# A causal mask moved into unused contraction rows: four 64x64 products on a diagonal block

## The reference, cut to what matters

```python
scores = jnp.einsum('bhqd,bhkd->bhqk', q, k) / math.sqrt(hd)
causal = jnp.tril(jnp.ones((l, l), bool))
scores = jnp.where(causal, scores, -jnp.inf)
att = jax.nn.softmax(scores, axis=-1)
out = jnp.einsum('bhqk,bhkd->bhqd', att, v)
```

## Time and profile before

| | us |
|---|---|
| three runs | 2000.06, 2002.21, 2006.18 (median 2002.21) |
| span of the profiled execution | 2000.6 |
| its time outside the span | not in the profile; the median run is 1.6 longer than the span |
| busy in the span: TensorE, VectorE, ScalarE, POOL | 1867.0, 1487.5, 1038.1, 635.2 |
| attention with its output projection | about 165 to 640 |

### The profile page before, as it was taken

The page is one execution under the profiler, slowest core; times in us unless marked ns, Lnnn a source line. Parts: engine busy times, 40 slices in busy tenths (PEclk is TensorE's granted clock), DMA queues, the critical chain, the costliest instruction groups (busy, mean ns, idle before and its releaser), DMA issues. The chain is left out here.

```text
span 2000.6 us, 40100 instructions
## 1 busy us (share of the span) xinstructions
PE 1867.0 (93%) x15312; PEld 1158.9 (58%) x15312; DVE 1487.5 (74%) x2424; ACT 1038.1 (52%) x1973; POOL 635.2 (32%) x812
## 2 busy tenths in 40 slices
PE   7998888998889789999999999999999999999989
PEld 3443333333334467775775766766676776757756
DVE  6567787888863215987888889888898898978931
ACT  4334777777773114644645636535635635546411
POOL 4685756576752111121112112121131121211221
PEclk9998999999999889999999999999999999999999
DMA  7875455455534403004030040132211121041000
GB/s 245 238 200 146 131 131 153 111 152 158 147 110 149 151 1 114 1 29 142 1 114 25 33 135 1 58 118 74 84 52 58 38 87 58 1 141 40 12 11 12
DMA packets 127215, 183.19 MB, mean 92 GB/s; under 512 B 46480, under 2 KB 83344, under 8 KB 127072
## 3 DMA queue, kind: packets, MB, share of 16 engines
q1 hardware_dynamic: 121072, 165.22, 27.0%
q0 software_dynamic: 4272, 12.91, 1.9%
q10 hardware_dynamic: 1728, 3.15, 0.4%
HBM read 147.39 MB, written 33.62 MB: 90 GB/s over the span
## 5 line engine op out<-in xcount | busy, mean ns | idle before, releaser
L1411 POOL TENSOR_TENSOR lohi<-h,lohi 128x256 f16<-128x256 f32 x224 | 173.7, 776 | 873.8 <-ACT lohi L1563 873.6
L1552 ACT ACTIVATE kept<-ax,T 128x1376 f16<-128x1376 f32 x248 | 357.0, 1439 | 122.5 <-DVE T L1626 116.6
L1620 DVE TENSOR_SCALAR_CACHE_REDUCE junk<-ax,T 128x1376 f16<-128x1376 f32 x248 | 406.4, 1639 | 2.7
L1067 ACT ACTIVATE pr<-s 128x512 f32<-128x512 f32 (+2 forms) x640 | 320.2, 553 | 94.7 <-PE s L956 73.9
L649 DVE TENSOR_REDUCE mx<-s 128x2 f32<-128x1024 f32 (+2 forms) x300 | 320.0, 1113 | 62.2 <-PE s L628 33.3
L1449 PE MATMUL ga<-xT_f,w_gate 128*128 128x256 f16 x2688 | 332.8, 274 | 7.5 <-DVE h L1677 4.6
L1459 PE MATMUL acc<-w_down,lohi 128*128 128x512 f16 x1344 | 326.4, 379 | 9.1 <-POOL lohi L1411 9.0
L1449 PE MATMUL ub<-xT_f,w_up 128*128 128x256 f16 x2688 | 332.2, 274 | 0.0
L1449 PEld LDWEIGHTS ga<-xT_f,w_gate 128*128 128x128 f16 x2688 | 262.9, 98 | 80.0 <-DVE h L1677 7.2
L1449 PEld LDWEIGHTS ub<-xT_f,w_up 128*128 128x128 f16 x2688 | 263.8, 98 | 31.9
L1677 DVE SCALAR_TENSOR_TENSOR h<-ub,g 128x256 f32<-128x256 f32 x224 | 94.1, 420 | 165.6 <-ACT g L1558 164.6
(11 more groups left out here) (177 smaller groups left out, 2668.0 us busy)
## 6 DMA issues: line engine op xcount, KB each, us to landing
ring<-wgu_scr SPq DMA_DIRECT2D x64, 688.0 KB, 5.3
ring<-wd_scr SPq DMA_DIRECT2D x24, 768.0 KB, 4.7
wgu_scr<-tk_h POOLq DMA_DIRECT2D x32, 172.0 KB, 2.8
q_scr<-qk_h SPq DMA_DIRECT2D x16, 256.0 KB, 2.6
k_scr<-qk_h SPq DMA_DIRECT2D x16, 256.0 KB, 4.4
v_scr<-v_f SPq DMA_DIRECT2D x16, 256.0 KB, 5.4
Q<-q_scr SPq DMA_DIRECT2D x64, 64.0 KB, 2.0
K<-k_scr SPq DMA_DIRECT2D x64, 64.0 KB, 2.0
```

What stands on the lines that cost most here:

```text
L1067: nc.scalar.activation(pr[:, g % NPR, NP * t + p0:NP * t + p1, 0:w], scores, ACT.Exp, scale=SCALE).then_inc(e2_ok, 1)
L1411: nc.gpsimd.tensor_tensor(hT[j % 2][:, 1, :], h[j % 2][:, :], hT[j % 2][:, 0, :], ALU.subtract).then_inc(hl_ok, 1)
L1552: nc.scalar.activation(kept[0][:, :], ax[k % 2][:, 1, :], ACT.Sign, scale=-1.0, bias=TF[:, 1:2], accum_out=cnt[:, 1:2]).then_inc(c1_ok, 1)
L1620: nc.vector.tensor_scalar(junk[:, :], ax[k % 2][:, 0, :], TF[:, 0:1], -float(KZERO), ALU.is_lt, ALU.add, accum_out=cnt[:, 0:1]).then_inc(c ...
```

## The change

The extra row of each head moves from partition 48 to 63, and the 15 partitions 48 to 62 get fixed steps: in Q, row m holds -60000 for queries below 64(m+1) and else 0; in K, row m holds 60000 for the 64 keys from 64(m+1) on and else 0. They are written once, since the loads of Q and K write partitions 0 to 47 only. A score product over 63 or 64 rows then carries -3.6e9 wherever a key's block of 64 lies behind the query's. What is left of a diagonal block are its two 64x64 blocks on the diagonal. For each, and for each of the two heads, a 64x64 piece of the identity times a 64x64 triangle is added (`mask`). `identx` and its transfers go.

```diff
@@ phase_project, TensorE, ahead of the first unit
-                        pe.wait_ge(sc.cst2, 64)
+                        pe.wait_ge(sc.cst, 6)
+                        pe.wait_ge(sc.one_in[0], 16 * 3 * NT)
@@ constants of the module
+NSTEP = L // RT - 1
+MR = KR + NSTEP
+STEP = 60000.0
@@ constants(), POOL
+        nc.gpsimd.memset(self.step_q[:, :], -STEP).then_inc(self.cst0, 1)
+        nc.gpsimd.memset(self.step_k[:, :], STEP).then_inc(self.cst0, 1)
...
+        nc.gpsimd.affine_select(out=self.step_q[:, :], in_=self.step_q[:, :], compare_op=ALU.is_ge, fill=0.0, base=RT - 1,
+                                pattern=[[-1, L]], channel_multiplier=RT).then_inc(self.cst, 1)
+        nc.gpsimd.affine_select(out=self.step_k[:, :], in_=self.step_k[:, :], compare_op=ALU.is_ge, fill=0.0, base=-RT,
+                                pattern=[[1, L]], channel_multiplier=-RT).then_inc(self.cst0, 1)
+        pool.wait_ge(self.cst0, 7)
+        nc.gpsimd.affine_select(out=self.step_k[:, :], in_=self.step_k[:, :], compare_op=ALU.is_ge, fill=0.0,
+                                base=2 * RT - 1, pattern=[[-1, L]], channel_multiplier=RT).then_inc(self.cst, 1)
@@ spread_constants(), SP
-        for t in range(NT):
-            a, c = slice(RT * t, RT * (t + 1)), slice(RT * (1 - t), P - RT * t)
-            sp.dma_start(self.identx[a, :], self.identb[c, :]).then_inc(self.cst2, 16)
-        for m in (self.mask_q, self.mask_k):
-            sp.dma_start(m[RT:P, :], m[0:RT, :]).then_inc(self.cst2, 16)
         for i in range(2):
             for t in range(NT):
-                r = RT * t + KR
+                for dst, src in ((self.Q[i], self.step_q), (self.K[i], self.step_k)):
+                    sp.dma_start(dst[RT * t + KR:RT * t + MR, :, :],
+                                 src[:, :].unsqueeze(1).broadcast_to([NSTEP, NP, L])).then_inc(self.one_in[i], 16)
+                r = RT * t + MR
                 sp.dma_start(self.K[i][r:r + 1, :, :], self.onerow[:, :]).then_inc(self.one_in[i], 16)
@@ new helper
+    def mask(self, o, mask):
+        for half in range(2):
+            for t in range(NT):
+                part = self.tile(half)
+                mm = self.nc.tensor.matmul(o[t][part, part], self.identb[self.tile(t), self.tile(t)],
+                                           mask[self.tile(t), self.tile(t)], start=False, stop=True)
+        return mm
@@ maxima_unit
-                rows = slice(RT * t, RT * t + KR)
+                rows = slice(RT * t, RT * t + MR)
...
-                for t in range(NT):
-                    nc.tensor.matmul(o[t][:, w - P:w], self.select(t, 0), self.mask_q[self.tile(t), :],
-                                     start=False, stop=False)
-                for t in range(NT):
-                    mm = nc.tensor.matmul(o[t][:, w - RT:w], self.select(t, 1), self.mask_q[self.tile(t), 0:RT],
-                                          start=False, stop=True)
+                mm = self.mask([o[t][:, w - P:w] for t in range(NT)], self.mask_q)
@@ shifted_pair
-                        rows = slice(RT * t, RT * t + KR + 1)
+                        rows = slice(RT * t, RT * t + MR + 1)
...
-                        for t in range(NT):
-                            nc.tensor.matmul(o[t][:, 0:RT], select(t, 0), mask_k[tile(t), RT:P], start=False, stop=False)
-                        for t in range(NT):
-                            mm = nc.tensor.matmul(o[t][:, 0:P], select(t, 1), mask_k[tile(t), :], start=False, stop=True)
+                        mm = sc.mask([o[t][:, 0:P] for t in range(NT)], sc.mask_k)
```

More of the change, by code:

```diff
@@ L538, in __init__ @@
         self.identb = sb("identb", [P, P], BF16)
-        self.identx = sb("identx", [P, P], BF16)
+        self.step_q = sb("step_q", [NSTEP, L], F16)
+        self.step_k = sb("step_k", [NSTEP, L], F16)
         self.mask_q = sb("mask_q", [P, P], BF16)
@@ L543, in __init__ @@
         self.cst = sem("cst")
-        self.cst2 = sem("cst2")
         self.qk_in = [[sem(f"qk_in{i}_{f}") for f in range(2)] for i in range(2)]
@@ L557, in constants @@
             nc.gpsimd.memset(t[:, :], 0.0).then_inc(self.cst0, 1)
-        pool.wait_ge(self.cst0, 4)
+        nc.gpsimd.memset(self.step_q[:, :], -STEP).then_inc(self.cst0, 1)
+        nc.gpsimd.memset(self.step_k[:, :], STEP).then_inc(self.cst0, 1)
+        pool.wait_ge(self.cst0, 6)
         nc.gpsimd.affine_select(out=self.identb[:, :], in_=self.identb[:, :], compare_op=ALU.not_equal, fill=1.0, base=0,
@@ L563, in constants @@
                                 pattern=[[-1, P]], channel_multiplier=1).then_inc(self.cst, 1)
-        nc.gpsimd.affine_select(out=self.mask_k[:, :], in_=self.mask_k[:, :], compare_op=ALU.is_ge, fill=MASKED, base=-RT,
+        nc.gpsimd.affine_select(out=self.mask_k[:, :], in_=self.mask_k[:, :], compare_op=ALU.is_ge, fill=MASKED, base=0,
                                 pattern=[[1, P]], channel_multiplier=-1).then_inc(self.cst, 1)
         nc.gpsimd.memset(self.mxT[:, :], 0.0).then_inc(self.cst, 1)
-    def spread_constants(self, sp):
-        sp.wait_ge(self.cst, 4)
-        for t in range(NT):
-            a, c = slice(RT * t, RT * (t + 1)), slice(RT * (1 - t), P - RT * t)
-            sp.dma_start(self.identx[a, :], self.identb[c, :]).then_inc(self.cst2, 16)
-        for m in (self.mask_q, self.mask_k):
-            sp.dma_start(m[RT:P, :], m[0:RT, :]).then_inc(self.cst2, 16)
+        nc.gpsimd.affine_select(out=self.step_q[:, :], in_=self.step_q[:, :], compare_op=ALU.is_ge, fill=0.0, base=RT - 1,
[5 more added lines that the diff above has]
+                                base=2 * RT - 1, pattern=[[-1, L]], channel_multiplier=RT).then_inc(self.cst, 1)
+    def spread_constants(self, sp):
+        sp.wait_ge(self.cst, 6)
         for i in range(2):
             for t in range(NT):
-                r = RT * t + KR
+                for dst, src in ((self.Q[i], self.step_q), (self.K[i], self.step_k)):
+                    sp.dma_start(dst[RT * t + KR:RT * t + MR, :, :],
+                                 src[:, :].unsqueeze(1).broadcast_to([NSTEP, NP, L])).then_inc(self.one_in[i], 16)
+                r = RT * t + MR
                 sp.dma_start(self.K[i][r:r + 1, :, :], self.onerow[:, :]).then_inc(self.one_in[i], 16)
@@ L608, in tile @@
         return slice(RT * t, RT * (t + 1))
-    def select(self, t, half):
-        return (self.identb if t == half else self.identx)[self.tile(t), :]
+    def mask(self, o, mask):
[5 more added lines that the diff above has]
+        return mm
     def maxima_unit(self, pe, s1, n, h, i, u):
@@ L692, in phase_attend @@
         qk_in, v_in, s1_ok, r1_ok, m_in = sc.qk_in, sc.v_in, sc.s1_ok, sc.r1_ok, sc.m_in
-        mask_k, tile, select = sc.mask_k, sc.tile, sc.select
         Va = [sb(f"Va{i}", [P, NB, QH, 2 * HD], F32) for i in range(2)]
@@ L863, in _ @@
                 nc.gpsimd.memset(Va[i][:, :, :, HD:2 * HD], 1.0).then_inc(sc.cst0, 1)
-            pool.wait_ge(sc.cst0, 6)
+            pool.wait_ge(sc.cst0, 9)
             pool.dma_start(bo_all[:, :], bo.unsqueeze(0).broadcast_to([P, D])).then_inc(b_ld, 16)
@@ L1017, in _ @@
             for i in range(2):
-                pe.wait_ge(sc.one_in[i], 16 * NT)
+                pe.wait_ge(sc.one_in[i], 16 * 3 * NT)
             slot(0, 0, 0, first=True)
```

## The result

The kernel after the change took 2044.42 us (median of four runs, 2042.15 to 2046.70); the kernel before, beside it, 2001.13 us (1997.56 to 2006.18). The ratio is 1.0215, with a 95% interval from 1.0192 to 1.0237: slower by about 43 us. The profiled execution has a span of 2045.0 us, 44.4 us longer than the one before.

A forecast was written before the change was run, and what follows sets the result against it. TensorE, 89% busy in mid-attention, was taken as the bound: 59 us more there, less 14 absorbed, plus 2 for set-up, on the 2000.6 us span gives 2047.6; with 1.6 around it, 2049 us, range 1990 to 2080.

The forecast's parts named there:

- The visit: Masking a diagonal block on TensorE, score behind: 0.09 us more going in, 0.12 to 0.15 instead of 0.09 after.
- The way out: TensorE leaving the 64x64 shape after the masks: 0.105 us taken, at most 0.15, which would add 23 us.
- another shape behind it: Mask visits followed by a product of another shape, about 115 of 512: 0.03 to 0.06 us more, 0.045 taken.
- The absorption: In attention, two thirds of TensorE's 21.4 us of waits for banks of scores, 14 us, outlast added work, leaving 45.
- latencies: TensorE's attention waits for the row of maxima (10.9 us), copied output (5.2) and joined maxima (4.0) stay.
- The group: Sign of being right: each of attention's 16 groups of heads gets longer by 2.5 to 4 us.
- TensorE's share: Sign of being right: TensorE is busy for more than 92% of the attention stage.
- The set-up: In the projections, SP's 12 transfers instead of 8 delay Q's stores by 2.4 us, 2 charged; POOL's extra work costs nothing.
- Free shape: Rival: the masks' 64x64 shape costs nothing, visits get 0.03 to 0.06 us shorter, around 1992 us; chance 0.17.
- Change as cheap as the columns: Rival: both shape changes of a mask visit cost some 0.03 us together, 1997 to 2008 us; chance 0.07.
- Four one after another: Rival: the four mask products run in sequence, 31 to 46 us on top, 2080 to 2100 us; chance 0.06.
- The feed-forward stages: Sign of being right: the stages after attention keep their length.

The follow-up runs named there:

- e1: The changed kernel with its four mask products writing all 128 output partitions, in the 64x128 shape of the scores, same 64 columns each; 2001.09 us, ratio 1.0000 to before.
- e6: As e1, but the maxima's masks use the change's four 64x64 pieces and the shifted scores keep the wide masks; 2020.25 us, ratio 1.0087 to before.
- e7: As e1, but the shifted scores' masks use the change's four 64x64 pieces and the maxima keep the wide masks; 2028.89 us, ratio 1.0150 to before.
- e3: As e2, and POOL makes the steps later, behind the first weights that it unpacks; 2033.41 us, ratio 1.0170 to before.
- e5: The changed kernel with the masks of e1 and the set-up of e3 together; 1990.84 us, ratio 0.9942 to before.
- e4: The changed kernel with both scores of a two-pair unit first, then both masks, 384 visits to 64x64 instead of 512; 2027.27 us, ratio 1.0126 to before.
- e2: The changed kernel with SP's twelve set-up transfers issued one each behind twelve stores later in the projections; 2037.87 us, ratio 1.0175 to before.

## Why the prediction was right, and where its sizes were off

It said 2049 us, in a range from 1990 to 2080; measured were 2044.42. The mechanism held: the shape of the masks, not their columns, decides, and TensorE is the engine that bounds the stage. The closeness of the number is luck: the visits cost 7 us more than forecast and the set-up 10 more, and 18 more were absorbed, which takes all of that back.

**The visit.** Forecast 0.12 to 0.15 us more, with a score behind; measured 0.16. The way in is the 0.09 that was taken from the earlier trace rows. The way out is 0.11, at the float16 pair's 0.105 in the earlier trace rows and not at the 0.15 behind float32. A bit low were the 0.12 to 0.15 from the first product to the next score: 0.16, which by e1 is 0.05 for the products and 0.11 for the way out. With another shape behind it is 0.09 + 0.15 instead of the 0.18 of before, so 0.06 more instead of 0.045. In the trace 381 of the 496 visits in attention have a score behind them and 115 another shape (I had counted 115 for all 512). That makes 381 x 0.155 + 115 x 0.06 = 66 us on TensorE, against 59 for all 512.

**The absorption: the step that failed.** I had 14 us absorbed, all of it from waits for banks, and wrote that the latencies "stay". Of the 66 us only 33.5 came through, so some 32 were absorbed. The waits for banks gave 6.5 us, less than half of the 14 (16.8 + 4.6 to 11.7 + 3.2). The two "latencies" gave 11.6: the row of maxima and the joined maxima are made by other engines while TensorE works, and a TensorE that comes later finds them there. With all smaller waits, TensorE's idle time between the two transposes fell by 20.4 us, from 64.1 to 43.7, and its recorded busy time rose by 53.9 (before, then after; the window, its length, and TensorE's busy time stand first):

```profile
164.88:675.18 510.30, 446.18 (x5409) 188.15 (x5409) 378.46 (x440) 344.88 (x686) 297.65 (x429) 0.96 0.50 142
```

```profile
176.54:720.30 543.76, 500.09 (x5409) 192.93 (x5409) 378.75 (x440) 344.18 (x686) 297.40 (x429) 0.97 0.47 133
```

So 12 of the 66 us are missing inside the recorded busy time. Both kernels have the same 5409 products here in the same order, so their starts can be compared one by one, from trace to trace. At the 385 visits where neither kernel waits and both run at the upper clock the change adds 55 us; where one of them waits, the time falls by 22; the rest cancels. What is missing is thus the price of the other 111 visits, which stand beside a wait or at the lower clock. Recorded ends can hide it: the masks of the earlier trace rows are recorded with 0.19 to 0.22 us, and the next score starts 0.09 us behind the first of them, so in front of a wait a longer visit uses up time that the profile had called busy. In the same way, behind the four scores at 386.29, two steps of 0.215 us, the next could have started at 386.72; it started at 387.06, and the profile calls only 0.17 of these 0.34 us idle. How much of the 12 us this makes up is not shown. e6 and e7 say that the absorption is no fixed stock of waits that the first visits use up.

**The group.** Forecast 2.5 to 4 us more for each of 16; measured 33.5 / 16 = 2.1, below the range that was to be a sign of being right, for the same reason. TensorE's share came above 92% (492.47 of the 525 us from 165 to 690 are 93.8%), as said.

**The set-up.** The place and the chain were right (SP's stores late, ScalarE waiting for them), the size was not: 2 us charged, 10.6 measured by e3. I had priced a transfer of fifteen rows like one of one row, 0.62 us; it holds SP for 0.85 to 1.33, so that the row of transfers grew by 5.0 us and not by 2.4. And the delay was not passed on one to one: TensorE stood 6.21 us (1.55 before) and then ran twelve products in 5.25 us instead of 2.75, at the lower clock. Nothing was charged for POOL, which was wrong by about 1.4 us: the idle 20.61 us of the earlier trace rows hide the time on POOL, but not what VectorE loses beside it.

**The rivals.** Free shape: fell by e1, though the saving that it named is real (e5). Change as cheap as the columns: fell by the 0.20 us. Four one after another: fell by e4; the four masks at 386.13 together are recorded with 0.22 us. The feed-forward stages kept their length.

## What to carry to other kernels

Price a small product by its change of shape, not by its columns: here a visit took 0.28 us in its neighbours' shape and 0.48 in another, with the same columns. Where the bounding engine waits for something that others make meanwhile, count that wait as room that added work can use, also where it looks like a latency: two of three such waits went here, the copied output's stayed. And price a one-time set-up by the queue that it stands in: what is behind it there, who waits for that, and what a stall of TensorE does to its clock afterwards.

## What the runs showed of the hardware that was not expected

- A change of which columns are used, with the rows equal (64x128 to 64x64), costs 0.09 us in and 0.11 out, as much as a change of rows.
- After TensorE had stood idle for 6.21 us, the granted clock was 0.51 for the next 6 us (1.2 GHz of 2.4), and twelve products took 5.25 us instead of 2.75. In e1, a stall of 5.24 us was followed by twelve in 4.44; in e2, without it, 2.75.
- VectorE's splits of weights took some 1.5 us each instead of 0.64 while POOL worked on the steps. POOL in order of time in the kernel after:

```profile
12.11 1.21 POOL L574 TENSOR_SCALAR_AFFINE_SELECT step_q<-step_q 15x1024 f16<-15x1024 f16 x1
13.28 1.48 POOL L576 TENSOR_SCALAR_AFFINE_SELECT step_k<-step_k 15x1024 f16<-15x1024 f16 x1
14.82 1.37 POOL L579 TENSOR_SCALAR_AFFINE_SELECT step_k<-step_k 15x1024 f16<-15x1024 f16 x1
```

The two slow splits start at 12.35, beside the first two of these; the next pair starts at 16.43, behind the last of them, and takes 1.27 us. The Trainium skill says so ("SBUF — State Buffer", SBUF: two separate sides): a VectorE operation with two inputs in SBUF and a POOL operation that reads SBUF hold a shared port in turn, and the other one waits. The splits have two such inputs, and e3 agrees. So does what follows them: the next two operations of VectorE (L382, at 15.23, beside the last select) take one of their inputs from PSUM, and with 1.27 us for the two they are no longer than before (1.41).
